# Attention in head groups: the four sets of exponentials times v in two steps of a hand-ordered schedule, in place of four

## The reference, cut to what matters

```
k, q, v = proj(W_key), proj(W_query), proj(W_value)        # each 16 heads x 512 x 16
scores  = einsum('bhqd,bhkd->bhqk', q, k) * hd ** -0.5      # causal mask, softmax over k
out     = einsum('bhqk,bhkd->bhqd', weight, v)              # "av" in the kernel
x       = layernorm(x + out @ W_proj.T * 256 ** -0.5)
x       = layernorm(x + moe(x))
```

## Time and profile before

| | |
|---|---|
| median of three runs | 985.91 us (981.85 to 986.39) |
| the profiled execution's own time | 987.11 us |
| span of the profile, first to last instruction | 985.4 us |
| PE busy in the span | 853.1 us (87%), mean granted clock 0.929 |
| DVE, ACT, POOL busy | 655.1, 524.4, 523.8 us |
| PE MATMUL of `st` (L607), `nat` (L622), `av` (L637) | 126.2, 128.6, 97.3 us busy |
| attention part | up to about 510 us of the span |

### The profile page before, as it was taken

How to read it: one execution, slowest core, us unless ns; L and a number is a source line. 1 busy time by engine, 2 the same in 40 slices (tenths; PEclk the granted TensorE clock), 3 DMA queues, 4 the chain that set the end, 5 groups by cost and what they waited for, 6 DMA issues and landing times. The chain is left out here.

```text
span 985.4 us, 17316 instructions
## 1 busy us (share of the span) xinstructions
PE 853.1 (87%) x6044; PEld 647.9 (66%) x6044; DVE 655.1 (66%) x1957; ACT 524.4 (53%) x994; POOL 523.8 (53%) x621
## 2 busy tenths in 40 slices
PE   4568899999999999888669599998989999898990
PEld 3334455564646454434359589998989989898990
DVE  4457677888787778889938974646464644646454
ACT  3026666657666656555518245554555546455555
POOL 5336565556565563323545527657474655747443
PEclk9669999999999999988859799998999989999995
DMA  4987667777776758310142314344242342512248
GB/s 132 161 156 120 118 120 140 141 140 141 134 136 103 132 104 145 128 41 2 44 150 76 112 23 65 77 92 118 47 116 36 79 92 33 135 29 38 39 125 249
DMA packets 90166, 100.26 MB, mean 102 GB/s; under 512 B 9056, under 2 KB 83552, under 8 KB 89952
## 3 DMA queue, kind: packets, MB, share of 16 engines
q1 hardware_dynamic: 72288, 77.66, 37.8%
q0 software_dynamic: 12800, 16.92, 10.2%
q10 hardware_dynamic: 4992, 4.59, 1.4%
HBM read 65.12 MB, written 33.62 MB: 100 GB/s over the span
## 5 line engine op out<-in xcount | busy, mean ns | idle before, releaser
L497 DVE CUSTOM_DVE_ANT_0 n_ps<-n_ps,tri 128x512 f32<-128x512 f32 (+3 forms) x512 | 237.2, 520 | 73.6 <-PE n_ps L622 72.3
L1055 DVE TENSOR_TENSOR h_lo<-g,h_hi 128x384 fp32r<-128x384 f32 (+1 forms) x184 | 138.1, 759 | 129.2 <-ACT h_hi L991 120.8
L411 ACT ACTIVATE pt<-st_ps 128x512 f32<-128x512 f32 x320 | 181.8, 603 | 77.1 <-PE st_ps L607 70.0
L1131 PE MATMUL y_ps<-w_parts,h_hi 128*128 128x256 f32 (+1 forms) x1152 | 212.4, 279 | 0.0
L986 ACT ACTIVATE g<-h_ps,b 128x384 f32<-128x384 f32 (+1 forms) x192 | 104.2, 543 | 195.5 <-PE h_ps L1117 159.6
L1117 PE MATMUL h_ps<-tt_hi,w_parts 128*128 128x384 f32 (+1 forms) x768 | 179.2, 338 | 30.6 <-issue 20.0
L359 POOL TENSOR_SCALAR_AFFINE_SELECT pt<-pt 128x256 f32<-128x256 f32 (+1 forms) x320 | 111.3, 361 | 147.4 <-ACT pt L411 145.9
L1131 PEld LDWEIGHTS y_ps<-w_parts,h_hi 128*128 128x128 f32 (+1 forms) x1152 | 171.8, 177 | 3.3 <-ACT h_hi L991 0.2
L958 POOL DMA_INDIRECT acc<-y,tok_no x64 | 103.1, 1611 | 117.1 <-DVE y L1069 106.4
L1131 PE MATMUL y_ps<-w_parts,h_lo 128*128 128x256 f32 (+1 forms) x576 | 160.6, 279 | 0.0
L1117 PEld LDWEIGHTS h_ps<-tt_hi,w_parts 128*128 128x128 f32 x768 | 134.1, 200 | 32.9 <-issue 31.7
(11 more groups left out here) (149 smaller groups left out, 1152.4 us busy)
## 6 DMA issues: line engine op xcount, KB each, us to landing
w_parts<-part_d SPq DMA_DIRECT2D x192, 128.0 KB, 6.6
w_raw<-in_w SPq DMA_DIRECT2D x16, 1024.0 KB
part_d<-w_raw SPq DMA_DIRECT2D x96, 128.0 KB, 7.4
w_raw<-in_xt SPq DMA_DIRECT2D x8, 512.0 KB, 4.5
res<-in_x SPq DMA_DIRECT2D x8, 512.0 KB, 10.8
x<-res SPq DMA_DIRECT2D x8, 512.0 KB, 6.6
acc<-res SPq DMA_DIRECT2D x8, 512.0 KB, 8.2
fin<-acc SPq DMA_DIRECT2D x4, 512.0 KB, 4.1
```

The lines of the kernel that those rows point to most:

```text
L411: nc.scalar.activation(pt[:, slot % PT_RING, n % UP, :], st_ps[at % ST_RING][:, :], ACT.Exp, scale=S_SCALE).then_inc(exp_done, 1)
L497: ins = nc.vector.tensor_tensor_reduce(out=src[:, h, :], in0=src[:, h, :], in1=mask, scale=-1.0, scalar=-BIG_NEG, op0=ALU.add, op1=ALU.min ...
L1055: nc.vector.tensor_tensor(h_lo[:, q % 2, n, 0:cols], g[:, at % G_RING, 0:cols], h_hi[:, q % 2, n, 0:cols].bitcast(F32), ALU.subtract).then ...
L1131: ins = nc.tensor.matmul(y_ps[at % Y_RING][0:rows, 0:C], x[:, q % 2, m, toks], w[e % 2][:, m, :], start=i == 0, stop=i == len(terms) - 1)
```

## The change

`AV_PLACES` gives the step of each of the four sets. Before, sets 0 to 3 stand in steps 4, 5, 6 and 7 of the group that follows theirs. After, sets 0 and 1 stand one behind the other in step 4, and sets 2 and 3 in step 6. The generator yields every set whose place is the step. Since ACT copies `av_ps` at the stage of set 3, its copy (L430) moves with it from step 7 to step 6, that is from behind the exponentials of step 7's unit to ahead of them. No instruction is added or removed, and no buffer changes.

```diff
-AV_PLACES = (4, 5, 6, 7)
+AV_PLACES = (4, 4, 6, 6)
...
                 group = i * GROUPS + g - 1
-                if k in AV_PLACES and 0 <= group < B * GROUPS:
-                    yield "av", group, AV_PLACES.index(k)
+                for n in range(TT):
+                    if k == AV_PLACES[n] and 0 <= group < B * GROUPS:
+                        yield "av", group, n
```

## The result

The median is 989.11 us after (987.08 to 991.09) and 983.92 us before (981.85 to 986.95), 11 executions each. The ratio that the executions give is 1.0035, with a 95% interval of 1.002 to 1.0049, which is 2 to 5 us; the medians themselves stand 5.2 us apart (0.53%), just outside it. So the change is slower, clear of zero, by some 3.5 to 5 us, about the 0.5% that I named. The forecast was 985.6 us and 0.3 us less than before. The profiled execution took 987.08 us, span 985.3 us. It is the shortest of its eleven and no longer than the one before (987.11), so the totals hide the loss and the stretches have to be read.

A forecast was written before the change was run, and what follows sets the result against it. PE is nearly full (50.09 of 51.93 us a pass), but waits on ACT and DVE chains decide. Group four +4.7, groups one to three -4.0, last passes -1.0 make -0.3 us: 985.6 us expected, range 974 to 993.

The forecast's parts named there:

- What a joined pair saves on PE: Each junction of two sets saves 0.22 us on PE, two per group; 13.6 us over 31 groups.
- first rival: PE's whole saving of 13.6 us stays, giving 972.3 us; chance 0.12.
- Group four: +0.94: Later nm and earlier av_sb copy delay ACT and DVE by 0.94 us a pass in passes 0 to 4.
- second rival: Group four costs less, some 0.2 us or 0, giving 981.9 or 980.9 us; chance 0.18.
- Groups one to three: -0.67: In passes 0 to 5 these groups gain 0.67 us a pass; group three's further gain is lost waiting for POOL.
- The pass: A repeating pass, logits to logits, takes 52.2 us in place of 51.93; wrong if under 51.3 or over 52.8.
- The 0 that I took for group four of pass 5: Group four of pass 5 costs nothing, since ACT is 0.95 us less loaded there and the delays vanish.
- The last passes: I take -0.5 us each: Passes 6 and 7 gain 0.5 us each, between 0 and -1.8.
- third rival: The copy ahead of step 7's unit costs in groups one to three too, giving 991.5 us; chance 0.22.
- fourth rival, the clock: Half-level clock behind the logits in four more passes, 1.48 us each, giving 991.5 us; chance 0.06.

The follow-up runs named there:

- e4: Kernel before with both pairs of sets joined only in group four of passes 0 to 5: 989.41 us, ratio 1.0030.
- e1: Kernel before with both pairs joined in all groups of passes 0 to 5 only, apart in passes 6 to 8: 985.54 us, ratio 0.9997.
- e3: Kernel before with both pairs joined only in groups one to three of passes 0 to 5: 977.98 us, ratio 0.9921.
- e11: Kernel before with both pairs joined only in groups one and two of passes 0 to 5: 980.71 us, ratio 0.9933.
- e2: Kernel before with both pairs joined in passes 6 to 8 only: 990.05 us, ratio 1.0044.
- e10: Kernel before with only sets 2 and 3 joined, in passes 6 to 8 only: 987.11 us, ratio 0.9996.
- e14: Kernel before with both pairs joined in group two of pass 6 only: 988.10 us, ratio 1.0032.
- e12: Kernel before with both pairs joined in pass 6 alone: 988.42 us, ratio 1.0014.
- e9: Kernel before with only sets 0 and 1 joined, in passes 6 to 8 only: 987.86 us, ratio 1.0009.
- e13: Kernel before with both pairs joined in groups one, three and four of pass 6 only: 986.03 us, ratio 1.0011.
- e15: Kernel before with both pairs joined in groups one to three of passes 0 to 5 and group one of passes 6 and 7: 978.02 us, ratio 0.9925.
- e7: Kernel before, all sets apart, with nm and logit ahead of the set in step 4 of group four: 999.61 us, ratio 1.0131.

## Why the prediction was wrong

**"What a joined pair saves on PE": right.** nm starts 1.52 us behind set 0 in place of 0.89, so 0.63 us later for a forecast of 0.66, and PE's busy time falls by 1.86 us in a pass (50.09 to 48.23) for eight junctions of 0.22 us, 1.76. The drain that the Trainium skill ("TensorEngine Tiling (Array Packing)", Key Properties) ties to a change of the tiling mode agrees with that, and it says nothing of the end: the whole saving is gone again in waits, so the first rival (972.3 us) fell.

**"Group four: +0.94": right.** Unit of step 9: 276.98 for a forecast of 276.97. Next pass's unit 277.65 for 277.63, DVE 277.63 for 277.65, PE's nat 279.55 for 279.61. By experiment: e4 against before is +0.84 in a pass, e1 against e3 +0.86 (52.00 and 51.14). The second rival, a smaller cost there, fell with it. PE's two waits, 0.82 and 0.42 us, are of the forecast's kind, though not its 0.6 to 0.8 each.

**"Groups one to three: -0.67": right for the profile after, small by 0.13 by experiment.** proj was 0.66 and x1 0.65 us early. e3 takes 51.13 us, 0.80 less than 51.93. Group three's own saving is lost in DVE's wait for POOL, which is still 2.31 us, but for the 0.09 us that e11 shows.

**The pass: right.** 52.19 us for a forecast of 52.2, 51.3 to 52.8 being the bounds I set. That it is exact to 0.01 us is luck: the four passes of this profile spread from 52.02 to 52.59, and e1's are 51.96 to 52.03. The 0 that I took for group four of pass 5 was -0.49 us (46.81 for 47.30 in e1 and e4).

**"The last passes: I take -0.5 us each": this step failed.** For the sum's -1.0 us the stretches show +4.4 (134.0 against 129.5), and it would be 4.9 without the 0.49 us that group four of pass 5 gives. e2, which joins only these passes, is slower by 0.44%, 4.4 us. I had not walked them. My bounds of 0 and -1.8 came from PE's saving alone and left a loss out. What the walk of pass 3 rests on is not there in pass 6. In group two, nm's wait for DVE took in set 1, and the qk behind step 7's unit covered the copy; without qk, which exists for passes up to 5 only, neither does, and group two costs 1.14 us up to proj, the two costs of group four. In group three, POOL has no cuts in front of its power, DVE's wait for it is 0.81 us in place of 2.95, and what set 1 delays reaches DVE and PE, which is 0.57 us late. The clock adds to both places. The third rival had one of these mechanisms (the copy ahead of the unit makes PE wait) and put it into the groups one to three of every pass. It does not hold there, since e3 is faster; it holds in group two of pass 6, where e10 shows it at 0.50 us and e14 shows the whole group at +3.1 us by its median.

**The fourth rival, the clock: right in kind, wrong in place.** It had the level fall behind the logits of more of the passes 0 to 5; in the profile after it falls there in none of four, and in the one before in two. It falls in group three of pass 6, and for 6.8 us in group two of pass 7, where before it fell for 3.4. In pass 6, the only falls that come with the joined sets are the ones in group three (five of five profiles with the first pair joined there) and at proj (e2, e12 and e14, but not after).

**What stays open.** Three things. What pass 7 costs by itself, which no run shows alone: the +1.6 us of e2 against e12 is from one profile each. Where e3's whole gain is from: 0.79% are 7.8 us, of which six passes at -0.80 give 4.8. In the seven profiles whose repeating passes are as before (before, e2, e9, e10, e12, e13, e14), 12 of 28 distances between logits are 53.4 in place of 51.9 us, with the clock at the half level; in e3 and e15 it is none of 8. 12/28 of 1.48 us in five passes are 3.2 us, which would fill the gap. But e11, which is as fast by its median, has three such distances of four in its profile (52.7 to 52.8 us; the execution is the longest of its eight, 984.13 us), so one profile of each kernel doesn't settle it. It may be the same that keeps the medians of e3 and e4 from adding up to e1's; that isn't shown. And what makes the clock fall in one execution and not in the next.

## What to carry to other kernels

When an edit is made by a loop, walk it through the iterations at the ends of the loop too: a stage that covers a delay in the steady state may not exist there, and here a change worth nothing in six passes went with a loss of 4.4 us in the last two. An edit that saves on a full engine is worth what it does to the chain of waits at each place, and it pays to make it place by place: joined in groups one to three of passes 0 to 5 it is worth 0.8%, joined everywhere it costs 0.35%. When one profile's total doesn't show what the medians show, compare it stretch by stretch with the parts that the change doesn't touch.

## What the hardware showed that I had not expected

TensorE's granted clock fell to the half level (0.50 in the windows above) in stretches where PE had waited for another engine for 0.3 to 1.2 us, up to some 5 us before the fall. One fall in a repeating pass cost 1.5 us (53.4 against 51.9), in e1 1.1 (53.10 against 52.00). The same order and the same waits do not always give the same level. The waits of 0.61, 0.37 and 0.92 us ahead of proj in pass 6 have it in e2, e12 and e14 and not in the kernel after. Two of four repeating passes of the kernel before have it (53.36, 53.39 us) and two not (51.93, 51.90), with the same 0.30 us wait of PE ahead of set 0; in one of them it came 3.2 us behind the start of the logits, some 5 us behind that wait. With 1.02 us of waiting ahead of the logits, e7 has it in five passes of five. It differs between executions of one kernel too: in e9's twelve the mean granted clock goes from 0.924 to 0.941 and the time from 991.9 to 984.6 us, the six at 0.928 or less all taking 988.9 us or more and the six at 0.934 or more 986.8 or less. An effect of 1 or 2 us is hard to tell from that in a few executions; the starts of rows on either side of the changed place tell it, as the first column of the table of pass 6 does.
